# Macaron block in one kernel: a new order of the beginning and the end, with the first two k products in plain fp32

## The reference

```python
def ffn(x):                         # on _layernorm(x), per sequence of 512 x 4 tokens
    x_prev = x shifted by one token, zero at a sequence's start
    xr = mu_r * x + (1 - mu_r) * x_prev
    xk = mu_k * x + (1 - mu_k) * x_prev
    r = sigmoid(xr @ W_r.T)
    k = xk @ W_k.T
    return r * (square(relu(k)) @ W_v.T)

def attn(x):                        # on _layernorm(x), 16 heads of 16
    q, k = relu(x @ Wq.T) / 4, relu(x @ Wk.T) / 4
    v, u = x @ Wv.T, silu(x @ Wu.T)
    kv = k.T @ v                    # per sequence and head, over all its tokens
    out = srms_norm(q @ kv) * u
    return out @ Wo.T

x = x + 0.5 * ffn(_layernorm(x))
x = x + attn(_layernorm(x))
x = x + 0.5 * ffn(_layernorm(x))
```

## Time and profile before

| | |
|---|---|
| median of 3 runs | 323.25 us |
| the profiled execution | 323.19 us |
| its span in the profile | 321.5 us |
| TensorE busy | 309.6 us (96%) |
| VectorE busy | 239.8 us (75%) |
| ScalarE busy | 239.7 us (75%) |
| GpSimd busy | 215.0 us (67%) |
| mean clock granted to TensorE | 1.00 |

### The profile page before, as it was taken

One profiled execution on the slowest core, in us unless ns is written; L12 is line 12 of the kernel. 1 busy time (PEld: TensorE's weight loads), 2 busy tenths in 40 slices (PEclk: granted clock), 3 DMA queues, 4 the chain that ended last, 5 costly groups with the idle time before them and its releaser, 6 DMA issues.

```text
span 321.5 us, 5807 instructions
## 1 busy us (share of the span) xinstructions
PE 309.6 (96%) x2052; PEld 280.2 (87%) x2052; DVE 239.8 (75%) x566; ACT 239.7 (75%) x465; POOL 215.0 (67%) x234
## 2 busy tenths in 40 slices
PE   6898999999999999999999999999999999998996
PEld 6677898899889988988988998889998989887985
DVE  3689984595675746895894797686989988995744
ACT  3698967969869679679259367479797979679861
POOL 4297858769778578669358217536687979797560
PEclk9999999999999999999999999999999999999999
DMA  7960000000000000000000000000002020121103
GB/s 215 352 219 0 3 1 0 2 0 2 0 1 3 0 2 0 0 2 0 2 2 0 2 0 2 0 3 1 2 1 67 0 67 0 66 67 66 65 2 131
DMA packets 11036, 10.85 MB, mean 34 GB/s; under 512 B 768, under 2 KB 11008, under 8 KB 11008
## 3 DMA queue, kind: packets, MB, share of 16 engines
q1 hardware_dynamic: 10432, 10.23, 9.8%
q10 hardware_dynamic: 576, 0.26, 0.3%
HBM read 6.29 MB, written 4.19 MB: 33 GB/s over the span
## 4 chain that ended last, share of the span: by engine, by line
PE 68%; DVE 15%; POOL 7%; issue 5%; ACT 4%; DMA 1%; SPq 0%; POOLq 0%; ACTq 0%
PE psK L1077 7%; PE psK L1078 7%; PE psK L1079 7%; PE psRV L1077 6%; PE psRV L1079 6%; PE psRV L1078 6%; PE psX L1078 6%; PE psX L1077 6%; PE psX L1079 6%; PE psK L1234 2%; PE psA L1094 2%; PE psX L1161 2%; PE psRV L1146 2%; DVE head_ss L892 1%; POOL gout L265 1%
## 5 line engine op out<-in xcount | busy, mean ns | idle before, releaser
L806 DVE SCALAR_TENSOR_TENSOR mix<-psA,mu,mix 128x512 f32<-128x512 f32 x64 | 44.0, 741 | 11.1 <-ACT mix L525 11.1
L359 POOL TENSOR_TENSOR mix_k_lo<-mix,mix_k_hi 128x512 fp32r<-128x512 f32 x30 | 39.2, 1328 | 12.9 <-ACT mix_k_hi L543 12.8
L525 ACT ACTIVATE mix<-psA,one_mu 128x511 f32<-128x511 f32 x64 | 39.5, 696 | 2.2 <-PE psA L1094 2.2
L512 ACT ACTIVATE xn<-xs,shiftA,rstdA 128x256 f32<-128x256 f32 x59 | 30.8, 603 | 12.4 <-POOL shiftA L343 12.4
L1077 PE MATMUL psRV<-ffn_hi,mix_r_hi 128*128 128x256 f32 x128 | 36.4, 284 | 0.0
L1079 PE MATMUL psRV<-ffn_hi,mix_r_lo 128*128 128x256 f32 x128 | 35.8, 279 | 0.0
L1078 PE MATMUL psRV<-ffn_lo,mix_r_hi 128*128 128x256 f32 x128 | 35.7, 279 | 0.0
L1077 PE MATMUL psK<-mix_k_hi,ffn_hi 128*128 128x512 f32 x64 | 26.1, 408 | 1.8 <-DVE mix_k_lo L961 1.5
L1077 PE MATMUL psRV<-ffn_hi,act_hi 128*128 128x256 f32 x96 | 27.5, 287 | 0.0
L1079 PE MATMUL psRV<-ffn_hi,act_lo 128*128 128x256 f32 x96 | 26.8, 279 | 0.0
L1078 PE MATMUL psRV<-ffn_lo,act_hi 128*128 128x256 f32 x96 | 26.8, 279 | 0.0
(11 more groups left out here) (157 smaller groups left out, 1066.3 us busy)
## 6 DMA issues: line engine op xcount, KB each, us to landing
xs<-x_dram SPq DMA_DIRECT2D x7, 512.0 KB, 8.7
out_dram<-xs SPq DMA_DIRECT2D x7, 512.0 KB, 2.9
out_dram<-xs SPq DMA_DIRECT2D x4, 128.0 KB, 1.7
xs<-x_dram ACTq DMA_DIRECT2D x2, 128.0 KB, 2.9
xs<-x_dram SPq DMA_DIRECT2D x2, 128.0 KB, 2.6
silu_u<-w_ffn_k_dram SPq DMA_DIRECT2D x1, 256.0 KB, 5.0
q_store<-w_k_dram SPq DMA_DIRECT2D x1, 256.0 KB, 5.2
silu_u<-w_ffn_r_dram SPq DMA_DIRECT2D x1, 256.0 KB, 6.5
```

The costliest lines, as they stand in the source:

```text
L359: nc.gpsimd.tensor_tensor(mix_k_lo[:, h, :], mix[:, 0, h, :], mix_k_hi[:, h, :].bitcast(F32), ALU.subtract).then_inc(s_lo_k, 1)
L512: nc.scalar.activation(xn[:, t, :], tile_row(xs, b, t), ACT.Identity, bias=shiftA[:, t:t + 1], scale=rstdA[:, t:t + 1]).then_inc(s_xn, 1)
L525: nc.scalar.activation(mix[:, rk, h, 1:BLOCK], psA[:, h, 0:BLOCK - 1], ACT.Copy, scale=one_mu[:, rk, h:h + 1]).then_inc(s_prev, 1)
L806: nc.vector.scalar_tensor_tensor(out=m, in0=psA[:, h, :], scalar=mu[:, rk, h:h + 1], in1=m, op0=ALU.mult, op1=ALU.add).then_inc(s_mix, 1)
```

## The change

- Passes 0 and 1: `ffn_k` uses plain fp32 matmuls of raw_ffn and mix; no high and low part of the k mix is made for them, and counts of s_hi_k and s_lo_k start with pass 2 (`k_parts`).
- Loads: W_k, x's block 1 and W_r come ahead of attention's weights, and W_v gets a buffer of its own name. mu is loaded as rows of 256 values, two small transposes on TensorE put it on the partitions, and VectorE copies it out of PSUM.
- TensorE's warm-up is 24 transposes, then mu's, then 6. The means of k and u come before `ffn_k(0)`, that of q before `ffn_v(0)`, that of v after `ffn_v(3)` (into psA).
- VectorE normalizes all tiles of pass 1 and tiles 0 and 1 of pass 2; it takes the statistics of pass 1 ahead of the mixes of pass 0. POOL makes two of the low weights and act_low(0).
- Middle: in passes 6 and 7 `add_attention` goes ahead of `stats_b`; `stats_a(9)` goes behind the mixes of pass 8; on POOL `x1_low(7)` and `kt_low(7)` go ahead of `scales_a(9)`; `r_low(8)` goes behind `keep_g(7)`.
- End: only pass 12 keeps the plain second product. Passes 13 to 15 split it; ACT writes relu and the high square, and a new `act_low2` on VectorE squares in psK and subtracts. `ffn_v` starts after the first half of its input. `ffn_k` of passes 14 and 15 runs over the contraction half outside. r_low of passes 13 and 14 is POOL's, of 15 VectorE's. ACT's second half of `previous` and the two sigmoids are interleaved. The last pass writes into psA and psK (`last_of`). `SPLIT_O` goes; as no block reached it, nothing else changes by that.

The diff, cut to its core:

```diff
-            sp.dma_start(raw_att[:, 0, :, :], weight_rows("k")).then_inc(s_w_in["k"], 16)
             load_x(1)
             sp.dma_start(raw_ffn[:, 1, :, :], weight_rows("ffn_r")).then_inc(s_w_in["ffn_r"], 16)
-            sp.dma_start(ffn_v_plain[:], weight_rows("ffn_v")).then_inc(s_w_in["ffn_v"], 16)
-            for n in (1, 2):
-                sp.dma_start(raw_att[:, n, :, :], weight_rows(ATT_W[n])).then_inc(s_w_in[ATT_W[n]], 16)
+            sp.dma_start(raw_att[:, 0, :, :], weight_rows("k")).then_inc(s_w_in["k"], 16)
+            sp.dma_start(raw_att[:, 1, :, :], weight_rows("u")).then_inc(s_w_in["u"], 16)
+            sp.dma_start(raw_ffn_v[:], weight_rows("ffn_v")).then_inc(s_w_in["ffn_v"], 16)
+            sp.dma_start(raw_att[:, 2, :, :], weight_rows("q")).then_inc(s_w_in["q"], 16)
             sp.dma_start(wv[:], weight_rows("v")).then_inc(s_w_in["v"], 16)
             load_x(2)
...
             scales_a(0)
-            pool.wait_ge(s_ffn_hi, 1)
             pool.wait_ge(*normalized(0, 2))
-            nc.gpsimd.tensor_tensor(ffn_lo[:, 0, :, :], raw_of(0), ffn_hi[:, 0, :, :].bitcast(F32),
-                                    ALU.subtract).then_inc(s_ffn_lo[0], 1)
+            for i in (0, 1):
+                pool.wait_ge(s_ffn_hi, i + 1)
+                nc.gpsimd.tensor_tensor(ffn_lo[:, i, :, :], raw_of(i), ffn_hi[:, i, :, :].bitcast(F32),
+                                        ALU.subtract).then_inc(s_ffn_lo[i], 1)
...
             scales_b(7)
+            x1_low(7)
+            norm_second(2)
+            kt_low(7)
             scales_a(9)
-            norm_second(2)
-            x1_low(7)
-            kt_low(7)
...
-            for n in range(8, LAST):
-                if n < SPLIT2:
...
+            norm_second(7)
+            scales_a(14)
+            add_ffn2(11)
+            k_low(13)
+            r_low(13)
+            scales_a(15)
+            add_ffn2(12)
+            k_low(14)
+            r_low(14)
+            add_ffn2(13)
+            k_low(15)
+            pool.wait_ge(s_lo_r, 2 * len(FFN))
             add_ffn2(14)
...
             def previous(n, halves=range(HALVES)):
-                act.wait_ge(s_lo_k, 2 * n)
+                if n <= 2:
+                    act.wait_ge(s_k, 2 * n)
+                else:
+                    act.wait_ge(s_lo_k, k_parts(n))
                 act.wait_ge(s_lo_r, 2 * n)
...
+                        act.wait_ge(s_act_lo, lows(n - 1))
                         act.wait_ge(s_v, 2 * n)
-                        act.wait_ge(s_act_lo, 2 * min(n, SPLIT2))
                     nc.scalar.activation(act_k[:, h, :], psK[:, h, :], ACT.Relu).then_inc(s_relu, 1)
                     act.wait_ge(s_relu, 2 * n + h + 1)
-                    if n < SPLIT2:
+                    if n != PLAIN:
                         nc.scalar.activation(act_hi[:, h, :], act_k[:, h, :], ACT.Square).then_inc(s_act_hi, 1)
-                        act.wait_ge(s_act_hi, 2 * n + h + 1)
-                    nc.scalar.activation(act_k[:, h, :], act_k[:, h, :], ACT.Square).then_inc(s_act, 1)
+                        if n < PLAIN:
+                            act.wait_ge(s_act_hi, lows(n - 1) + h + 1)
+                    if n <= PLAIN:
+                        nc.scalar.activation(act_k[:, h, :], act_k[:, h, :], ACT.Square).then_inc(s_act, 1)
             def sigmoid_r(n, g):
...
-                mix_high(n + 1, 1)
-                if n + 2 <= LAST:
+                if n + 2 < 14:
                     normalize(n + 2)
-            activate_k2(LAST)
-            sigmoid_r(LAST, 0)
-            sigmoid_r(LAST, 1)
+            activate_k2(12)
+            sigmoid_r(12, 0)
+            sigmoid_r(12, 1)
+            previous(13, (0,))
+            keep_g_rows(7)
+            previous(13, (1,))
+            mix_high(13, 0)
+            normalize(14)
+            mix_high(13, 1)
+            activate_k2(13)
+            previous(14, (0,))
+            sigmoid_r(13, 0)
+            previous(14, (1,))
+            sigmoid_r(13, 1)
+            mix_high(14, 0)
+            normalize(15)
+            mix_high(14, 1)
+            activate_k2(14)
+            previous(15, (0,))
+            sigmoid_r(14, 0)
+            previous(15, (1,))
+            sigmoid_r(14, 1)
+            mix_high(15, 0)
+            mix_high(15, 1)
+            activate_k2(15)
+            sigmoid_r(15, 0)
...
+            def act_low2(n):
+                for h in range(HALVES):
+                    dve.wait_ge(s_act_hi, lows(n - 1) + h + 1)
+                    nc.vector.scalar_tensor_tensor(out=psK[:, h, :], in0=psK[:, h, :], scalar=0.0, in1=act_k[:, h, :],
+                                                   op0=ALU.max, op1=ALU.mult).then_inc(s_act, 1)
+                    dve.wait_ge(s_act, 2 * (n - NB) + h + 1)
+                    nc.vector.tensor_tensor(act_lo[:, h, :], psK[:, h, :], act_hi[:, h, :].bitcast(F32),
+                                            ALU.subtract).then_inc(s_act_lo, 1)
...
             stats_a(0)
+            dve.wait_ge(s_mu_t, 1)
+            nc.vector.tensor_copy(mu[:].rearrange("p r h -> p h r"),
+                                  psK[:, 0, 0:2 * HALVES].rearrange("p (h r) -> p h r", r=2)).then_inc(s_mu, 1)
+            dve.wait_ge(s_mu, 1)
+            nc.vector.tensor_scalar(one_mu[:], mu[:], -1.0, 1.0, ALU.mult, ALU.add).then_inc(s_one_mu, 1)
             normalize_some(0)
-            dve.wait_ge(s_mu_in, 32)
-            nc.vector.tensor_scalar(one_mu[:], mu[:], -1.0, 1.0, ALU.mult, ALU.add).then_inc(s_one_mu, 1)
...
+            stats_a(1)
+            for rk in range(2):
+                for h in range(HALVES):
+                    mix_one(0, rk, h)
             next_column(0)
-            ffn_weight_low(1)
-            center_weight("k", 1)
+            normalize_some(1)
+            r_low(0)
+            center_weight("k", 2)
+            center_weight("u", 2)
+            ffn_weight_low(2)
+            mix_current(1)
+            center_weight("q", 3)
             stats_a(2)
...
+            r_low(1)
             gate_ffn(0, 0)
+            normalize_some(2)
             add_ffn1(0, 0)
-            r_low(1)
             gate_ffn(0, 1)
             add_ffn1(0, 1)
...
             x2_low(7)
-            stats_a(9)
             keep_g(6)
             mix_current(8)
+            stats_a(9)
             projections(7)
             g_low(2)
             gate_heads(3)
-            r_low(8)
             add_attention(2)
             keep_g(7)
+            r_low(8)
             stats_a(10)
...
+            gate_ffn(11, 0)
+            gate_ffn(11, 1)
+            add_attention(6)
+            head_norms(7)
+            stats_a(14)
+            mix_current(13, (0,))
+            g_low(7)
+            mix_current(13, (1,))
+            gate_ffn(12, 0)
+            gate_ffn(12, 1)
+            add_attention(7)
+            stats_a(15)
+            act_low2(13)
+            mix_current(14)
+            gate_ffn(13, 0)
+            gate_ffn(13, 1)
+            act_low2(14)
+            mix_current(15)
             gate_ffn(14, 0)
             gate_ffn(14, 1)
+            r_low(15)
+            act_low2(15)
+            for g in range(2):
+                dve.wait_ge(s_gate, 2 * LAST + g + 1)
             finish_last()
...
-                for m in range(HALVES):
+                def part(m, c):
+                    if m == 0:
+                        pe.wait_ge(s_hi_k, k_parts(n) + c + 1)
+                        pe.wait_ge(s_lo_k, k_parts(n) + c + 1)
+                    last = product(psK[:, m, :], ffn_hi[:, 0, c, tok(m)], ffn_lo[:, 0, c, tok(m)],
+                                   mix_k_hi[:, c, :], mix_k_lo[:, c, :], c == 0, c == HALVES - 1)
+                    if c == HALVES - 1:
+                        last.then_inc(s_k, 1)
...
+                if n < 2:
+                    pe.wait_ge(s_w_in["ffn_k"], 16)
+                    for m in range(HALVES):
+                        for c in range(HALVES):
+                            if m == 0:
+                                pe.wait_ge(s_mix, mix_part(n, 0, c))
+                            last = nc.tensor.matmul(psK[:, m, :], raw_ffn[:, 0, c, tok(m)], mix[:, 0, c, :],
+                                                    start=(c == 0), stop=(c == HALVES - 1))
+                        last.then_inc(s_k, 1)
+                elif n in (14, LAST):
                     for c in range(HALVES):
...
+                        for m in range(HALVES):
+                            part(m, c)
+                else:
+                    for m in range(HALVES):
+                        for c in range(HALVES):
+                            part(m, c)
...
             def ffn_v(n):
-                pe.wait_ge(s_act_lo, 2 * n + 2)
+                if n == LAST:
+                    pe.wait_ge(s_halo, n + 2)
                 for t in range(TILES):
-                    if t % 2 == 0:
+                    dst = psRV[:, t // 2, (t % 2) * D:(t % 2 + 1) * D]
```

(51 more changed lines are left out.)

200 lines of the change are left out of this document (62 added, 138 removed).

## The result

The changed kernel takes **317.57 us** (median of 5 runs, 317.32 to 318.14); the kernel before took 323.16 us in the same comparison (median of 5). The ratio is 0.983, 95% interval 0.982 to 0.985: by it 5.4 us faster, 1.7%. The prediction had 320.4 us and a range of 318.5 to 322.7. The profiled execution of after took 318.14 us, its span is 316.4 (before: 321.5).

What follows compares the result with a forecast made beforehand. The prediction took TensorE's work, plus a beginning and a tail, to bound the kernel. Its terms -2.0 + 0.87 - 0.87 - 0.8 gave -2.8 us: span 318.7, time 320.4 us, range 318.5 to 322.7.

Steps and rivals of the forecast that it cites:

- Middle: New order around block 7: gram(7) no longer stops for POOL's k_lo; -0.87 us, bounds 0 and -0.9.
- mean v: Mean of w_v on TensorE moves from the shadow of act_lo to behind v(3), losing its cover: +0.87 us.
- Beginning: Up to T_B(0), the transposes of x1's block 0: second part at 30.45 against 32.48 us, -2.0 us (-3.0 to -1.2).
- End: Blocks 13 to 15, split v in place of plain, up to the last addition: -0.8 us, bounds +0.5 and -1.6.
- Rival B: No company cost: VectorE's passes stay at 0.69 beside POOL, the end gives 1.4; time 318.8 us, chance 0.13.
- C: Beginning: mu or ffn_r late by 0.8 us, passed on by VectorE's in-order queue; time 322.2 us, chance 0.14.
- D: Beginning: TensorE's clock stays or falls back at 1.2 GHz; +2.1, time 325.3 us, chance 0.10 with other losses.

Runs made afterwards that it cites:

- square_in_sbuf: Changed kernel with act_low2 of blocks 13 to 15 writing its relu-square to act_k in SBUF instead of psK: 319.18 us, ratio 0.9889.
- pairs: Separate test kernel, six VectorE passes per stage beside four POOL subtractions: with two SBUF inputs VectorE 1.40 us for 0.69, POOL 1.60 for 1.26.
- no_warm_up: Changed kernel without its 30 warm-up transposes (24 ahead of mu's, 6 behind): 318.07 us, ratio 0.9854 to the kernel before.

## Why the prediction was right or wrong

**Middle, mean v: right.** The stop of 0.87 us went as forecast; 0.17 us came on top from block 6. mean v cost 0.75 to 0.76 for 0.87, and 0.1 more went in k(4) behind it.

**Beginning: right in mechanism, a term mis-sized.** VectorE's row decides T_B(0), as the prediction said. It had T_B(0)'s second part at 30.45; it was 29.13. From xn(1) to the last addition the prediction counted 14.2 to 30.4, 16.2 us; the trace has 14.05 to 29.07, 15.0 us. The 1.2 us are three things. 0.45 is the first addition, priced at 1.05 beside att_lo; it took a step of 0.60, since it came ahead of att_lo (26.70 for 26.87), and it was POOL's three passes that got longer (4.59 us, where two undisturbed take 2.55). Some 1.05 is passes priced at their durations or a little above, where the step from start to start counts: xn(1) 1.45 for 1.29, r_low(0) 1.45 for 1.21, the centering of q with stats_a(2) 2.55 for 2.19, and so on over about 30 passes. Against these stands a wait of 0.30 for rstdA that I had not seen. The other 0.15 us is the row's start. Plain k ran 3.4 us a block for the 3.35 counted.

**End: the failing step, company that had moved away.** The sum followed the trace (shifted by 3.58 us) to v(13) within 0.05 us. Then r(14) was 0.46 early, v(14) 0.64, r(15) 0.97, the last addition 0.7. "lo at 297.5 and 298.9" and r_low(14)'s end at 301.8 have POOL's pairs at 2.9 us each, the price in the earlier trace rows (2.96). They ran 2.56 and 2.53. The price was measured beside VectorE's r_low of the same block, a difference of two SBUF inputs:

```profile
297.21 2.52 DVE L826 TENSOR_TENSOR mix_r_lo<-mix,mix_r_hi 128x512 fp32r<-128x512 f32 x2 [2.54 <-ACT mix_r_hi L543]
```

The change gives r_low(14) to POOL itself, so no such pass was left beside k_low(14), and the prediction kept the price. k(14) starts 0.39 us sooner than counted: 0.25 is that k_low(14) found its input earlier, the rest the shorter pass; r(14), behind r_low(14), 0.46 sooner. How that becomes 0.97 at r(15) isn't taken apart here. What VectorE does beside k_low(14) now is a mix and two gates, each with an operand in PSUM. Its new pairs aren't the reason: the prediction priced them rightly (0.68 a pass), none of them runs beside a k_low, and with both operands in SBUF k_low took the same time (square_in_sbuf). pairs shows the company's price alone, 1.60 for 1.26; no run puts r_low(14) back on VectorE, so this cause rests on the traces and not on a run of its own.

**End: the pace of the last tiles.** The prediction gave VectorE 0.86 us per tile and said that finishing is VectorE's pace. In the kernel before that was TensorE's: a plain tile is four records 0.215 us apart, and VectorE's gates start 0.87 apart behind them.

```profile
316.33 0.84 PEld L1146 LDWEIGHTS psRV<-ffn_v_plain,act_k 128*128 128x128 f32 x4
317.20 0.84 PEld L1146 LDWEIGHTS psX<-ffn_v_plain,act_k 128*128 128x128 f32 x4
```

With the split's 0.70 a tile VectorE runs at its own pace, 0.80 (311.04, 311.84, 312.64, 313.43), and the four tiles take 3.26 us for the 3.5 counted.

**The common cause.** The prediction took prices from rows of before without asking whether what set them would still stand beside the pass: the addition was priced beside att_lo and ran ahead of it, the low parts beside a r_low that had gone, the last tiles at the pace of a plain TensorE. It took company, too, as a property of POOL's being busy; its own trace had the counterexamples, the gates with psRV and the mixes with psA, which kept 0.68 beside POOL. Rival B (318.8) went furthest in this direction, with a chance of 0.13; even it had VectorE's row 0.4 us too long and the end at 1.4.

**Rivals C and D.** mu and ffn_r were late by little, one_mu done at 8.7 for the 8.4 counted, w_r with ScalarE at 9.6 for 9.0, and VectorE's row passed nothing on: xn(1) started 0.15 early. TensorE's clock was at the upper level at T_A(0), though the 24 warm-ups had all run at the lower one; before, the spacing halves at 7.6 us and not at 7.4. The price of the lower one is 1.7 us (no_warm_up) and not the 4.9 that D had, because the clock rose by k(0).

## What to carry to other kernels

Before pricing a VectorE pass beside POOL, look at its operands and at what will really stand beside it in the new order. One input in PSUM kept both engines at their pace; two in SBUF (or a tensor_scalar) cost up to twice the time, more for a single pass that is caught. Sum an engine's row by steps between starts, never by durations. Before carrying over a pace, ask which engine set it. Work moved into another engine's gap is free only if the two don't hold each other up while it runs, and a low part moved on POOL must be checked against what it then queues behind. Compare two traces from a point behind the warm-up.

## What the runs showed of the hardware

- VectorE alone 0.69 us for 128x512 of fp32, 1.40 beside POOL with two SBUF inputs, POOL 1.26 and 1.60; a VectorE pass caught by POOL's addition took 1.79, and a tensor_scalar of 128x4 behind POOL's difference 1.28 for 0.17.
- A plain fp32 record of 512 columns takes 0.43 us, two per matmul, 3.4 us a block of k; the split block takes 2.80.
- Without warm-ups TensorE reached the upper clock by k(0) at 13.1 us, after eight transposes and two means. With them the spacing of the transposes halved at 6.3, 7.6 and 8.5 us in three traces that all began the warm-up at 2.60.
- From T_A(0) to T_B(0)'s second part the same kernel repeats to 0.01 us; ahead of it the same warm-up took 4.37 to 4.98 us (24 transposes) and 6.66 to 7.21 (forty).
